# The first attention's output pipeline: another order on three engines, no filling products, and a scan that reads PSUM

## The reference, cut to what matters

```
q, k = elu(q) + 1, elu(k) + 1
kv = einsum('nshd,nshm->nhmd', k, v);  ksum = sum(k, axis=1)
z = 1 / (einsum('nlhd,nhd->nlh', q, ksum) + 1e-6)
t = einsum('nlhd,nhmd,nlh->nlhm', q, kv, z)
x1 = layer_norm(t + x, ln1_g, ln1_b)
h = gelu(x1 @ W1.T + b1);  y = h @ W2.T + b2
out = layer_norm(y + x1, ln2_g, ln2_b)
```

## Time and profile before

| | us |
|---|---|
| median of three runs | 5587.15 |
| the profiled execution, own time | 5590.89 |
| its span in the profile | 5588.9 |
| granted clock over the span, share of full | 0.866 |
| first instruction of `mix0` on TensorE | 262.08 |
| first gathered block after it | 522.33 |

### The profile page before, as it was taken

How to read it: one execution, slowest core, us unless ns; L and a number is a source line. 1 busy time by engine, 2 the same in 40 slices (tenths; PEclk the granted TensorE clock), 3 DMA queues, 4 the chain that set the end, 5 groups by cost and what they waited for, 6 DMA issues and landing times.

```text
span 5588.9 us, 75596 instructions
## 1 busy us (share of the span) xinstructions
PE 4056.0 (73%) x18105; PEld 2830.9 (51%) x18105; DVE 3567.1 (64%) x10862; ACT 2783.9 (50%) x5993; POOL 3285.7 (59%) x3443
## 2 busy tenths in 40 slices
PE   3997776666662596577777776578777776797998
PEld 3554554544442595355555554456555554333565
DVE  5377766666667666577777776677777786622111
ACT  2365666666662232477777776544444442343222
POOL 0124777777774755677777776477777777012222
PEclk9998878778875598799888987798999998898999
DMA  4293555455541344445444444344444444200110
GB/s 129 67 280 102 144 140 140 138 140 140 140 131 48 108 139 128 138 135 135 135 136 136 136 136 115 109 131 133 133 133 133 133 133 129 86 23 28 34 34 27
DMA packets 349460, 658.87 MB, mean 118 GB/s; under 512 B 80930, under 2 KB 198704, under 8 KB 348760
## 3 DMA queue, kind: packets, MB, share of 16 engines
q0 software_dynamic: 156336, 433.90, 28.6%
q1 hardware_dynamic: 182928, 211.64, 12.8%
q10 hardware_dynamic: 9772, 8.50, 0.5%
HBM read 539.67 MB, written 115.45 MB: 117 GB/s over the span
## 4 chain that ended last, share of the span: by engine, by line
PE 20%; POOL 16%; issue 16%; DVE 9%; DMA 8%; ACT 1%; DVEq 1%; POOLq 0%; SPq 0%; ACTq 0%
POOL AR L1001 11%; DMA AR<-D_z,SRCI 7%; PE ps L1229 4%; PE ps L2669 4%; PE ps L2650 4%; PE ps L2357 3%; DVE AR L1088 2%; POOL AR L1685 2%; PE ps L2369 1%; POOL D_sx L1675 1%; DVE AR L1115 1%; POOL AR L1813 1%; DVE AR L1093 1%; PE ps L2273 1%; DMA D_sx<-AR 1%
## 5 line engine op out<-in xcount | busy, mean ns | idle before, releaser
L1001 POOL DMA_INDIRECT AR<-D_z,SRCI x1856 | 1777.5, 958 | 637.0 <-issue 498.1
L1229 PE MATMUL ps<-AR 128*128 128x264 f32 (+2 forms) x5568 | 1706.8, 459 | 359.5 <-DVE AR L1088 140.3
L1229 PEld LDWEIGHTS ps<-AR 128*128 128x128 f32 x5568 | 1209.1, 226 | 690.1 <-issue 286.8
L1001 POOL DMA_INDIRECT AR<-D_h,SRCI x904 | 870.0, 962 | 277.3 <-issue 246.2
L1115 DVE TENSOR_TENSOR AR<-ps,AR 128x264 f32 (+2 forms) x1392 | 588.0, 422 | 161.2 <-DVE AR L1115 136.0
L1276 ACT ACTIVATE AR<-iota_n,NREL 128x128 f32<-128x128 f32 x1856 | 587.6, 389 | 29.6 <-PE ps L1229 26.2
L1093 DVE TENSOR_TENSOR AR<-AR,ps 128x1024 f32<-128x1024 f32 x464 | 558.3, 1203 | 0.1
L1034 DVE TENSOR_TENSOR AR<-AR 128x128 f32<-128x128 f32 (+2 forms) x174 | 49.0, 282 | 674.6 <-SPq L982 674.4
L1287 ACT ACTIVATE AR<-AR,iota_p 128x1024 bf16<-128x1024 bf16 x348 | 394.7, 1134 | 21.0 <-DMA AR<-D_rel 21.0
L1289 ACT ACTIVATE AR<-AR,ones 128x1024 bf16<-128x1024 bf16 x348 | 399.5, 1148 | 11.4
L1293 ACT ACTIVATE AR<-ps 128x128 f32<-128x128 f32 (+2 forms) x174 | 47.1, 271 | 594.2 <-PE ps L1195 589.0
(11 more groups left out here) (446 smaller groups left out, 7700.2 us busy)
## 6 DMA issues: line engine op xcount, KB each, us to landing
AR<-D_rel SPq DMA_DIRECT2D x348, 256.0 KB
D_sx<-AR SPq DMA_DIRECT2D x8, 6370.0 KB
AR<-D_z,SRCI POOLq DMA_INDIRECT x1856
AR<-D_h,SRCI POOLq DMA_INDIRECT x928
D_y<-AR SPq DMA_DIRECT2D x106, 128.0 KB, 1.7
AR<-in_L_ffn_Wd SPq DMA_DIRECT2D x8, 1024.0 KB, 12.2
AR<-D_mask SPq DMA_DIRECT2D x58, 128.0 KB
D_h<-AR SPq DMA_DIRECT2D x49, 132.0 KB, 1.7
```

What stands on the lines that cost most here:

```text
L1001: e.indirect_dma_start(out=GV[:, u % 48, :], out_offset=None, in_=D_row[L.i], in_offset=bass.IndirectOffsetOnAxis(ap=SRCI[:, u:u + 1], axi ...
L1229: t = e.matmul(banks[n % 3][:, 0:YW], Sr[:, u % 8, :], GV[:, u % 48, L.GW - YW:L.GW], start=(i == 0), stop=(i == 1))
```

## The change

Three things are changed in `mix0`. On TensorE `keep_warm` is gone, `narrow` is split in halves and these stand between the attends, so that `turn`, `project` and `widen` come last in a round. On ScalarE `gelu` moves to the start of the next round, and `turned` and `falling` go behind `centre`. On VectorE `join` and `features` go to the end of a round, behind `narrowed` and `coefficients`, and `join` handles a group one round earlier than before. A wait of VectorE for its own semaphore is added for the single-tile group. In the passes ScalarE's copy into `TSC` is gone: the first scan and the subtraction read `BK_T` in PSUM.

```diff
@@ -659,20 +659,13 @@
             return [range(i, min(i + 2, nb)) for i in range(0, nb, 2)]
 
         def mix0_tensor(e):
-            def keep_warm(g, times):
-
-                if g >= 2:
-                    e.wait_ge(h0_ready, 2 * g - 2)
-                for _ in range(times):
-                    e.matmul(banks[4][:, 0:512], ident[:, :], NREL[:, 0:512], start=True, stop=True)
-
-            def attend(g):
+            def attend(g, tiles):
                 b0, nb = GROUPS[g]
                 e.wait_ge(q_ready, 2 * g + 2)
-                for i in range(nb):
+                for i in tiles:
+                    if i >= nb:
+                        return
                     b = b0 + i
-                    if i >= 2:
-                        keep_warm(g, 3 if i == 2 else 1)
                     if b >= 2:
                         e.wait_ge(att_taken, b - 1)
                     for j in range(2):
@@ -708,33 +701,41 @@
                         t = e.matmul(banks[4 + m][:, 0:w], W1m[:, k, 128 * m:128 * m + 128], x1T[:, k, 0:w], start=(k == 0), stop=(k == 1))
                     t.then_inc(h0_ps, 1)
 
-            def narrow(g):
+            def narrow(g, p):
 
                 b0, nb = GROUPS[g]
+                if p >= len(halves(nb)):
+                    return
                 e.wait_ge(h0_ready, 2 * g + 2)
                 e.wait_ge(x1b_ready, g + 1)
-                for p, pr in enumerate(halves(nb)):
-                    if g:
-                        e.wait_ge(y0_taken, 4 * g - 2 + 2 * p)
-                    for i in pr:
-                        o = banks[6 + p][:, 256 * (i % 2):256 * (i % 2) + 256]
-                        for k in range(2):
-                            e.matmul(o, hT0[g % 2][:, k, 128 * i:128 * i + 128], W2m[:, k, :], start=(k == 0), stop=False)
-                        for k in range(2):
-                            t = e.matmul(o[:, 128 * k:128 * k + 128], x1b[g % 2][:, k, 128 * i:128 * i + 128], ident[:, :], start=False, stop=(k == 1))
-                    t.then_inc(y0_ps, 1)
+                if g:
+                    e.wait_ge(y0_taken, 4 * g - 2 + 2 * p)
+                for i in halves(nb)[p]:
+                    o = banks[6 + p][:, 256 * (i % 2):256 * (i % 2) + 256]
+                    for k in range(2):
+                        e.matmul(o, hT0[g % 2][:, k, 128 * i:128 * i + 128], W2m[:, k, :], start=(k == 0), stop=False)
+                    for k in range(2):
+                        t = e.matmul(o[:, 128 * k:128 * k + 128], x1b[g % 2][:, k, 128 * i:128 * i + 128], ident[:, :], start=False, stop=(k == 1))
+                t.then_inc(y0_ps, 1)
 
             for r in range(-1, NGR + 2):
-                if 0 <= r < NGR:
-                    attend(r)
-                if 0 <= r - 1 < NGR:
+                now, one, two = 0 <= r < NGR, 0 <= r - 1 < NGR, 0 <= r - 2 < NGR
+                if now:
+                    attend(r, (0, 1))
+                if two:
+                    narrow(r - 2, 0)
+                if now:
+                    attend(r, (2,))
+                if two:
+                    narrow(r - 2, 1)
+                if now:
+                    attend(r, (3,))
+                if one:
                     turn(r - 1)
                 if r + 1 < NGR:
                     project(r + 1)
-                if 0 <= r - 1 < NGR:
+                if one:
                     widen(r - 1)
-                if 0 <= r - 2 < NGR:
-                    narrow(r - 2)
             meet(e, 4)
 
         def mix0_scalar(e):
@@ -781,18 +782,18 @@
                     e.activation(x1[:, :], x1[:, :], ACT.Identity, bias=nb1[g % 2][:, i:i + 1], scale=rs1m[g % 2][:, i:i + 1]).then_inc(x1_ready, 1)
 
             for r in range(-1, NGR + 3):
-                if 0 <= r - 1 < NGR:
-                    turned(r - 1)
-                if r + 1 < NGR:
-                    falling(r + 1)
-                if 0 <= r - 1 < NGR:
-                    gelu(r - 1)
+                if 0 <= r - 2 < NGR:
+                    gelu(r - 2)
                 if 0 <= r < NGR:
                     spread(r, ln1_var, ln1_std, mv1[r % 2], sd1)
                 if 0 <= r - 3 < NGR:
                     spread(r - 3, ln2_var, ln2_std, mv2[(r - 3) % 4], sd2)
                 if 0 <= r < NGR:
                     centre(r)
+                if 0 <= r - 1 < NGR:
+                    turned(r - 1)
+                if r + 1 < NGR:
+                    falling(r + 1)
             meet(e, 4)
 
         def mix0_vector(e):
@@ -865,19 +866,21 @@
                     e.wait_ge(y0_taken, b0 + nb)
                     e.sem_inc(ln2_var, 1)
 
-            for r in range(-1, NGR + 4):
+            for r in range(-1, NGR + 3):
                 if 0 <= r < NGR:
                     attended(r)
-                if 0 <= r - 4 < NGR:
-                    join(r - 4)
-                if r + 1 < NGR:
-                    features(r + 1)
+                    if GROUPS[r][1] < 4:
+                        e.wait_ge(ln1_var, r + 1)
                 if 0 <= r - 2 < NGR:
                     narrowed(r - 2, 0)
                 if 0 <= r < NGR:
                     coefficients(r)
                 if 0 <= r - 2 < NGR and GROUPS[r - 2][1] > 2:
                     narrowed(r - 2, 1)
+                if 0 <= r - 3 < NGR:
+                    join(r - 3)
+                if r + 1 < NGR:
+                    features(r + 1)
             meet(e, 4)
 
         def mix0_gpsimd(e):
...
@@ -1039,8 +1042,8 @@
                 K = L.k0 + k
                 mk = MKr[K % 2]
                 e.wait_ge(mk_in[K % 2], 48 * (K // 2 + 1))
-                e.wait_ge(t_there, K + 1)
-                e.tensor_tensor_scan(B1[0:P, :], mk[0:P, 0, :], TSC[0:P, :], -BIG, ALU.add, ALU.max).then_inc(*dv.up())
+                e.wait_ge(t_ps, K + 1)
+                e.tensor_tensor_scan(B1[0:P, :], mk[0:P, 0, :], BK_T[0:P, 0:128], -BIG, ALU.add, ALU.max).then_inc(*dv.up())
                 e.wait_ge(*dv.now())
                 e.tensor_tensor_scan(B2[0:P, ::-1], mk[0:P, 1, ::-1], B1[0:P, ::-1], -BIG, ALU.add, ALU.max).then_inc(run_ready, 1)
 
@@ -1076,7 +1079,7 @@
                 e.wait_ge(*dv.now())
                 e.scalar_tensor_tensor(out=B2[0:P, :], in0=mk[0:P, 3, :], scalar=BK_T[0:P, 385:386], in1=B2[0:P, :], op0=ALU.add, op1=ALU.max).then_inc(*dv.up())
                 e.wait_ge(*dv.now())
-                e.tensor_tensor(B2[0:P, :], TSC[0:P, :], B2[0:P, :], ALU.subtract).then_inc(x_ready, 1)
+                e.tensor_tensor(B2[0:P, :], BK_T[0:P, 0:128], B2[0:P, :], ALU.subtract).then_inc(x_ready, 1)
 
             def weigh(g, q):
 
@@ -1288,10 +1291,6 @@
                 e.wait_ge(*ac.now())
                 e.activation(OHr[v], OHr[v], ACT.Relu, bias=ones[:, 0:1], scale=-1.0).then_inc(oh_ready, 1)
 
-            def turned(k):
-                e.wait_ge(t_ps, L.k0 + k + 1)
-                e.activation(TSC[0:P, :], BK_T[0:P, 0:128], ACT.Copy).then_inc(t_there, 1)
-
             def weights(k):
                 K = L.k0 + k
                 w = BK_W[L.i][K % 2]
@@ -1308,8 +1307,6 @@
             one_hot(0, 1)
             for g in range(-1, NG2):
                 k = g + 1
-                if k < NG2:
-                    turned(k)
                 if g >= 0 and not L.weighted:
                     spread(g, 1)
                 side.after_spread1(e, k)
```

More of the change, by code:

```diff
@@ L905, in program @@
         mk_in = [sem(f"mk_in{i}") for i in range(2)]
-        rows_there, oh_ready, ad_ps, e_ready, t_ps, t_there, run_ready, edge_ps, row_ready, col_ps, x_ready, ex_ready, al_ps = [
-            sem(n) for n in ("rows_there", "oh_ready", "ad_ps", "e_ready", "t_ps", "t_there", "run_ready", "edge_ps", "row_ready", "col_ps", "x_ready", "ex_ready", "al_ps")]
+        rows_there, oh_ready, ad_ps, e_ready, t_ps, run_ready, edge_ps, row_ready, col_ps, x_ready, ex_ready, al_ps = [
+            sem(n) for n in ("rows_there", "oh_ready", "ad_ps", "e_ready", "t_ps", "run_ready", "edge_ps", "row_ready", "col_ps", "x_ready", "ex_ready", "al_ps")]
         assert AR.at <= 25608
@@ L922, in program @@
         OHr = AR.ring(2, 1024, dt=BF16)
-        AD, TSC, B1, B2 = [AR.take(128) for _ in range(4)]
+        AD, B1, B2 = [AR.take(128) for _ in range(3)]
         RL, RF, FW, BW = [AR.take(140) for _ in range(4)]
```

## The result

| | before | after |
|---|---|---|
| median, us | 5588.17 | 5617.23 |
| lowest and highest of five runs | 5586.58 to 5591.22 | 5616.19 to 5618.17 |
| span of the profiled execution | 5588.9 | 5614.3 |
| `mix0`: first product to the first gather behind it | 260.25 | 290.41 |
| the passes: that gather to the span's end | 5066.6 | 5063.1 |

What follows compares the result with a forecast made beforehand. The prediction took `mix0` to be bound by an 18.99 us loop of waits between VectorE and TensorE. Stage +26.4, clock +2 and copy -1 summed to +27.4 us, forecast 5615 us, range 5601 to 5632.

Steps and rivals of the forecast that it cites:

- `mix0` decides, the passes carry it through: Whole kernel: what `mix0` gains or loses goes nearly whole into the time, since the gathers start behind it.
- The filling products fill a gap; removed: 0: TensorE in `mix0`: four products, 3.4 us a round, fill time waiting for VectorE; removing them changes 0.
- Fourth tile 1.6 us late: `mix0`, new order: `narrow` between the attends delays the fourth tile, 1.6 us of new VectorE wait a round.
- ScalarE does all behind VectorE; `features` waits 3 us for the Exp: `mix0`, new order: ScalarE runs `centre` to Exp in a row, VectorE waits some 3 us; round 21.2 us against 18.99.
- The clock, 2 us, bounds 0 and 21.6: TensorE in `mix0`: standing still 4.5 us each round halves its clock, slowing `widen`; +2 us, bounds 0 and 21.6.
- covered while it ends there: Slow `widen` ends at 21.3 us, before `gelu`'s second half starts at 21.6, so its 1.8 us costs nothing.
- The clock rival: Half rate reaches `narrow` in every round of `mix0`: 21.6 us in place of 2, 5634 us; chance 10%.
- The stage: All of `mix0`: groups 0 to 2 +6.5 us, groups 2 to 12 +21.9, then the rest -2; sum +26.4.
- The end: `mix0` from group 12 on: `join` a round earlier lets less hang there; -2 us, bounds -6 and +2.
- The copy, -1: The passes: ScalarE's copy leaves and PSUM is read instead; -1 us, bounds -2.5 and +1.
- PE is the bound: Rival: TensorE's 98% busy is the real limit of `mix0`; round 16.1 us, -35 us, 5552 us; chance 5%.
- Tile 3 in time: Rival: `gelu` and `narrow` don't hold up the fourth attend; 1.6 us a round less, 5599 us; chance 10%.

Runs made afterwards that it cites:

- e12_no_fill_again: Kernel before without its filling products, order unchanged, a repeat timing: +15.8 us against the kernel before, ratio 1.0028.
- e9: Kernel after with nine filling products added on TensorE between `project` and `widen`: +22.4 us against the kernel before, ratio 1.004.
- e4: Kernel after with TensorE's four attends ahead of both halves of `narrow`: round 19.26-19.51 us; ratio to the kernel before 1.0012 (0.9982-1.0041), on a slow chip.
- e10: Kernel after with nine filling products between `project` and `widen`, and Relu for Exp in `falling`: +12.7 us against the kernel before, ratio 1.0022.
- e8: Kernel before without filling products and copy, TensorE doing `project` and `turn` ahead of the third attend, `widen` between `narrow`'s halves: -41.3 us, ratio 0.9926.
- e1_copy_only: Kernel before with only the copy into `TSC` taken out of the passes: ratio 1.0033 (0.9998-1.0067) against the kernel before, on a slow chip.
- e11_copy_only_again: Kernel before with only the copy into `TSC` taken out of the passes, timed on another chip: -2.6 us, ratio 0.9996 (0.9987-1.0005).

## Why the prediction was right, point by point

Forecast +27.4 us, measured +29.1; the place, the sign and the main mechanism were right. That the sum came so near is partly luck: terms were off by up to 4.3 us and cancelled.

**`mix0` decides, the passes carry it through.** Right. +30.2 in `mix0` came out as +25.4 in the span and +29.1 in the medians.

**The filling products fill a gap; removed: 0.** Wrong as a step. Their time did lie in a gap, and with them gone the old order lost 15.8 us (e12_no_fill_again), since they had kept the clock up for `turn` and `project`. In the new order the gap lies elsewhere, between `project` and `widen`, and costs less.

**Fourth tile 1.6 us late.** Right: 1.54 by e9 less e4. On VectorE it began 7.47 us into the round in e9, where I had 7.5, and 6.84 in the kernel after. There the first tile itself was 0.66 late, and the first half of `narrow` ran at 0.39 us and not at 1.1: with the attends late, `gelu` was done before PE got there.

**ScalarE does all behind VectorE; `features` waits 3 us for the Exp.** Right: 2.68 us, no gap from `centre` to `gelu`, and the removed load shortens the round by 1.27 (e10 against e9). The loop without the clock is 20.89 us against 21.2 forecast, and 19.35 against 19.6 without the fourth tile's wait. That VectorE's new order or ScalarE's alone would do the same was not tried.

**The clock, 2 us, bounds 0 and 21.6.** The mis-sized term: at least 6.3 us (e9). The mechanism was as described, down to `widen` taking the slow stretch, and the step "covered while it ends there" is what failed. I compared the end of `widen` with its reader `gelu`, which did have time, and not with what follows it in TensorE's own order, the next group's attends, which `features` had made ready at 408.27, 0.82 us before `widen` let them start. My own items had it: `features` ends at 20.4, the slow `widen` at 21.3. I also took one `widen` as 1.8 us longer, from a `project` of 5.40 us; in every third or fourth round the clock came back only about when it ended, and it took 6.59 to 6.75. The clock rival (+21.6) stays false: in no round does the half rate come to `narrow`, only the last, single-tile one ran at 0.50 (at 540.71).

**The stage.** Groups 0 to 2: +6.5 forecast, +4.9 measured. I had put the square root's table load, 1.28 us, behind `attended` in both rounds; ScalarE did it long before (in the first at 266.36, the square root itself at 276.49). Groups 2 to 12: +21.9 and the 2 for the clock, +26.7 measured. The last of these rounds, forecast at 19.4 us, took 21.44: the single tile's `features` was done at 514.49, but its attend stood behind a slow `widen` of 5.78 us and began at 517.69. The end: -2 forecast, -0.2 measured; no run moved `join` by itself, so what it brought is open. Ahead of group 0 the first `project` fell at full clock this time (3.70 us against 5.40), -1.2, which the change does not touch: luck. The errors partly cancel: -1.6, +2.8, +1.8, -1.2.

**The copy, -1.** By the traces about -2.2, inside the bounds, with overlapping sets; by the medians not distinguishable from nothing.

**The rivals.** "PE is the bound" is refuted by e12: without its filling products TensorE waits 33.5 of 180 us for VectorE, and the old order slows. With the same work on TensorE in another order the round falls from 20.5 to 15.60 us (e8). The "98% busy" in that rival is of one round; over `mix0` it is 91% (234.77 of 257 us). "Tile 3 in time" would have given a round of 19.35 us, not 19.6, and did not happen.

**What stays open.** Why the clock returns inside `widen` in most rounds and only behind it in every third or fourth. No kernel varied the gap's length by itself. No kernel changed VectorE's or ScalarE's order alone either; their part is shown by the removed Exp and by the waits.

## What to carry to other kernels

Ask of every slowed instruction who stands behind it on its own engine, not only who reads its result. Before filling products are taken out, see whose clock they keep up: put real work into that gap, as e8 does, and they are not needed. When filling products are put in, look at the last rounds as well: nine of them gave 6.3 us and took 2.0 back. And in a software pipeline (a loop in which the engines work on different groups at once) first write down the loop of waits with its sum; here moving `project` and `turn` ahead of the third attend gave 41 us where shifting work on three engines lost 29.

## What the runs showed of the hardware that was not expected

Two waits of 2.44 and 1.23 us on TensorE, with one attend of 0.72 us between them, were enough for a granted clock of 0.50 (e12_no_fill_again). The Trainium skill (TensorE: Matmul & The Clock Gate, section "Why this matters for your kernels") names idle gaps between bursts of matmuls as the cause of the half rate. This trace agrees on the cause, but each of its gaps is shorter than those that the row warns of; the measurement decides.

One table load less on ScalarE's path gave the load's row, 1.27 us a round against 1.28: no more hangs on it than it shows.

One chip differed in the gathers and not in `mix0`. In e1_copy_only GpSimd's gathers waited 419.6 us for a releaser, "remote", that all four traces of that chip name (417.7 to 425.6 us) and none of the other ten, and longer for TensorE. Idle time ahead of the gathers' line there, us and times:

```profile
  remote: 419.6, 198
  PE ps L1229: 359.2, 165
```

In e11_copy_only_again, the same kernel on another chip:

```profile
  PE ps L1229: 56.0, 181
```

The kernel took 6398 us there and 5587 here. What "remote" stands for was not tried.
